# Eight scatters around the RMS factors split two and six, ranks inside the second layer, half a normed x moved to the head of the odd steps

## The chip, the cores and the metric

The kernel runs as one launch on one core of a Trainium2 chip. The metric is the time of one execution on the device in microseconds (us); smaller is better. The core's engines run side by side and meet only at semaphores: TensorE (PE: matrix products, with its weight loads shown as PEld), VectorE (DVE), ScalarE (ACT), GpSimd (POOL) and SyncE (SP, which only starts DMA transfers). Each engine works through its own instructions in order.

## What is computed

A layer norm, a graph layer with a residual, a second layer norm and a mixture of eight experts with a residual, for 8 batches of 1024 tokens of width 128:

```python
def gnn(x, adjacency, epsilon, W1, b1, rms_weight, W2, b2):
    agg = epsilon * x + einsum('bnm,bmd->bnd', adjacency, x)
    h = einsum('bnd,dh->bnh', agg, W1) + b1                 # hidden width 512
    h = silu(h * rsqrt(mean(h * h) + 1e-6) * rms_weight)
    return einsum('bnh,hd->bnd', h, W2) + b2

def ffn(x, Wg, bg, W1, b1, W2, b2):                         # 8 experts, 2 chosen for each token
    scores = einsum('bsd,ed->bse', x, Wg) + bg
    top, idx = top_k(scores, 2);  p = softmax(top)
    return sum over the two chosen e of p_e * (relu(x @ W1[e].T + b1[e]) @ W2[e].T + b2[e])

x = x + gnn(layernorm(x), adj, ...)
x = x + ffn(layernorm(x), ...)
```

## The kernel before

The 8192 tokens are cut into NG = 16 groups of 512 tokens (GT = 4 tiles of 128), two groups to a batch. The program has two parts. The **first part** does the graph layer and the choice of experts and ends with a scatter of every token's normed row to the two experts' places in the DRAM buffer `slots`. The **second part** takes `slots` in 71 tiles of 256 rows through the expert weights. The change touches only the first.

The first part is a software pipeline of 16 steps (`first_part`, `step(g, par, b)` on each engine, par = g % 2, b = g // 2). In step g, group g is multiplied by the adjacency (`M(0)` to `M(7)`, L545, eight pieces between which the other work of TensorE is laid), group g-1 goes through the hidden layer, group g-2 through the second layer norm, gate and ranks, and group g-3 is scattered. What one step does for group g-1 is a ring through all engines:

- VectorE adds the second layer's result of the group before into `x_all` (`add_second_layer`, L1079). I count a step from the start of one L1079 to the start of the next; step 10 is the one from 206.5 to 229.8 us.
- VectorE then takes the second layer norm's statistics (`ln2_stats`, L1018, L1023), adds b1 to the first layer's result (`add_b1`, L1003), and writes the normed rows (`normed_rows`, L1030), which TensorE transposes (`transpose_normed`, L502) for the gate (`gate`, L509).
- GpSimd turns the statistics into factors (`ln2_factors`, L850, L851: an addition and a power), sends four of the eight scatters of group g-3 (`scatter_rows`, L884), computes the RMS factors of group g-1 (`rms_factors`, again L850, L851) from ScalarE's sums of squares (`sum_squares`, L700), and sends the other four. Each scatter is followed by a piece of other work: in odd steps a fill (`rest_by_fill`, L871), in even steps one eighth of the addition of b2 to a batch of x (`rest_by_b2`, L877). At the end of an even step it computes the first layer norm's factors of the next batch (`ln1_factors`, L855 to L858).
- VectorE and ScalarE scale the hidden values, half each (`scale_hidden`, L1038, L705). TensorE transposes them (`transpose_hidden`, L495, 16 matmuls), ScalarE applies silu (`hidden`, L714), and TensorE does `M(6)`, the ranks (`rank`, L515 and L519, which wait for VectorE's choices), `M(7)` and the second layer (`second_layer`, L529, 32 matmuls).

ScalarE also makes the normed x of the next batch (`normalise`, L691) in the odd steps: one half behind `scale_hidden`, the other behind `hidden`; it waits for `ln1_factors`. It rounds the aggregate (L748) and, in steps 4 to 11, the high part of an expert's first weights (`high_weights`, L684), of which VectorE makes the low part (`low_weights`, L987) at the end of the same step, behind `add_second_layer`. The adjacency of group g+2 is loaded by SyncE (2 MB) when `M(7)` of group g is over. `normed_rows` and `places` wait until the scatters of the group two before, which used the same buffers, have landed.

## Time and profile before

| | |
|---|---|
| median of three runs | 653.26 us (652.2 to 655.01) |
| the profiled execution, whole | 647.74 us |
| its span, first to last instruction | 646.0 us |
| TensorE busy | 562.3 us (87%) |
| GpSimd busy | 408.7 us (63%) |
| VectorE busy | 352.0 us (54%) |
| ScalarE busy | 294.7 us (46%) |
| mean granted TensorE clock | 0.949 |

The profile comes from one execution. Its page gives the busy time of each engine, the chain of work that ended last (followed back from the last instruction through whatever released each step) and the costliest groups of instructions. The trace behind it can be asked for the waits, for the timeline of one engine and for the busy time and granted clock of any stretch. In a timeline row the first number is the start in us from the beginning of the span, the second the duration; "x4" means four instructions merged into the row; the bracket says how long the engine stood idle before and what released it.

### The profile page before, as it was taken

To read this page: it belongs to the slowest core of one execution; us is meant where nothing else is said; L and a number is where in the kernel's file an instruction comes from. 1 tells how busy PE (TensorE), PEld (TensorE's weight loads), DVE (VectorE), ACT (ScalarE), POOL (GpSimd) and SP (SyncE) were. 2 spreads that over 40 slices of the span, in tenths; PEclk is the share of its full clock that TensorE was granted. 3 is DMA by queue.
4 is the path that set the end of the run, shared out by engine and by line. 5 is a ranking of instruction groups with operands and counts; after the bars stand their busy time and mean duration, and the time that the engine had idled before them with its cause. 6 is when DMAs were issued, how large, how long until landed. Compare 5 with 4: busy or idle time off the path is not lost.

```text
span 646.0 us, 13035 instructions
## 1 busy us (share of the span) xinstructions
PE 562.3 (87%) x3704; PEld 463.3 (72%) x3704; DVE 352.0 (54%) x1174; ACT 294.7 (46%) x779; POOL 408.7 (63%) x664
## 2 busy tenths in 40 slices
PE   1999878978798789888985899999999999999882
PEld 0467655655466457555764889999999999999850
DVE  2566665765765757554636474445444444544454
ACT  3354544536345445363342345544554554455411
POOL 5244596477664864775566588776667667667750
PEclk9999879999998799889786899999999999999998
DMA  8995414432344134324010567766767666766698
GB/s 364 334 417 214 151 34 150 152 127 92 122 156 150 35 146 151 104 90 148 17 34 21 205 213 265 254 246 253 256 237 258 258 239 237 265 247 242 217 408 365
DMA packets 40519, 127.18 MB, mean 197 GB/s; under 512 B 7776, under 2 KB 19809, under 8 KB 38273
## 3 DMA queue, kind: packets, MB, share of 16 engines
q1 hardware_dynamic: 31232, 108.88, 45.8%
q0 software_dynamic: 8640, 16.93, 7.9%
q8 instruction: 32, 0.52, 0.3%
q10 hardware_dynamic: 576, 0.53, 0.3%
q14 instruction: 39, 0.31, 0.2%
HBM read 61.19 MB, written 24.02 MB: 132 GB/s over the span
## 4 chain that ended last, share of the span: by engine, by line
PE 57%; POOL 17%; issue 8%; DVE 7%; DMA 5%; ACT 4%; SPq 2%; POOLq 0%; ACTq 0%; DVEq 0%
POOL slots L884 10%; PE ps_y L529 9%; PE ps_y L651 8%; PE ps_g L651 8%; PE ps_agg L545 7%; PE ps_t L495 3%; PE ps_h L495 3%; POOL rms_rstd L851 2%; PE ps_agg L638 2%; PE ps_agg L637 2%; PE ps_h L637 2%; PE ps_h L641 2%; PE ps_agg L641 2%; PE ps_h L638 2%; PE ps_t L626 2%
## 5 line engine op out<-in xcount | busy, mean ns | idle before, releaser
L951 POOL DMA_INDIRECT parts<-adj_in x142 | 138.6, 976 | 68.8 <-ACT adj_in L796 52.4
L545 PE MATMUL ps_agg<-adj_in,xn_both 128*128 128x512 f32 x256 | 137.5, 638 | 13.0 <-ACT xn_both L691 13.0
L884 POOL DMA_INDIRECT slots<-rows,dest x128 | 132.0, 1032 | 23.4 <-issue 23.4
L796 ACT ACTIVATE adj_in<-adj_in,share 128x128 f32<-128x128 f32 x142 | 49.4, 395 | 117.3 <-issue 104.4
L700 ACT ACTIVATE hn<-hb 128x512 f32<-128x512 f32 x64 | 40.0, 625 | 83.4 <-DVE hb L1003 83.4
L651 PE MATMUL ps_y<-W2e,hb 128*128 x576 | 70.2, 275 | 0.8 <-issue 0.8
L1215 DVE TENSOR_TENSOR xe_split<-ps_t,xe_split 128x256 fp32r<-128x256 f32 x71 | 30.1, 425 | 73.5 <-ACT xe_split L778 71.3
L651 PE MATMUL ps_g<-W2e,hn 128*128 x560 | 68.1, 275 | 0.0
L651 PEld LDWEIGHTS ps_y<-W2e,hb 128*128 128x128 f32 x576 | 67.3, 192 | 1.0 <-issue 1.0
L545 PEld LDWEIGHTS ps_agg<-adj_in,xn_both 128*128 128x128 f32 x256 | 46.5, 207 | 29.5 <-issue 26.9
L651 PEld LDWEIGHTS ps_g<-W2e,hn 128*128 128x128 f32 x560 | 65.4, 191 | 0.0
L529 PEld LDWEIGHTS ps_y<-consts,siluT 128*128 128x128 f32 x512 | 59.6, 192 | 7.3 <-issue 7.3
L850 POOL TENSOR_TENSOR ve<-mv,ln_eps 128x4 f32<-128x4 f32 x16 | 3.2, 199 | 91.9 <-DVE mv L1023 91.9
L529 PE MATMUL ps_y<-consts,siluT 128*128 128x128 f32 x512 | 59.8, 275 | 0.0
L495 PE MATMUL ps_h<-ident,hn 128*128 128x128 f32 x128 | 23.1, 340 | 36.3 <-ACT hn L705 36.3
L495 PEld LDWEIGHTS ps_h<-ident,hn 128*128 128x128 f32 x128 | 18.5, 173 | 48.0 <-DVE hn L1038 47.5
L871 POOL MEMSET rest_of_pool<- 128x128 f32 x222 | 50.1, 226 | 0.2
L637 PE MATMUL ps_agg<-xe_split,wcur 128*128 128x256 f32 x142 | 45.7, 322 | 0.0
L1038 DVE TENSOR_SCALAR hn<-hb,rms_rstd 128x512 f32<-128x512 f32 x32 | 14.1, 483 | 54.5 <-POOL rms_rstd L851 54.5
L705 ACT ACTIVATE hn<-hb,rms_rstd 128x512 f32<-128x512 f32 x32 | 21.3, 713 | 44.5 <-POOL rms_rstd L851 44.5
L637 PE MATMUL ps_h<-xe_split,wcur 128*128 128x256 f32 x142 | 40.0, 282 | 0.0
L638 PE MATMUL ps_agg<-xe_split,wcur 128*128 128x256 f32 x142 | 39.9, 281 | 0.0
(179 smaller groups left out, 1242.0 us busy)
## 6 DMA issues: line engine op xcount, KB each, us to landing
wcur<-expert_w SPq DMA_DIRECT2D x71, 578.0 KB
adj_in<-in_adjT SPq DMA_DIRECT2D x16, 2048.0 KB, 8.4
adj_in<-slots SPq DMA_DIRECT2D x71, 130.0 KB
expert_w<-parts SPq DMA_DIRECT2D x8, 512.0 KB, 9.4
out<-x_all SPq DMA_DIRECT2D x8, 512.0 KB, 7.0
x_all<-in_x SPq DMA_DIRECT2D x1, 3072.0 KB, 23.8
parts<-adj_in POOLq DMA_INDIRECT x142
expert_w<-in_F1T SPq DMA_DIRECT2D x1, 2048.0 KB, 19.4
```

Of the source, the lines that this page charges most:

```text
L495: ins = pe.transpose(h_bank[c][:, j * P:(j + 1) * P], hn[:, j, c * P:(c + 1) * P], ident[:, :])
L529: ins = pe.matmul(ps_y[:, j * P:(j + 1) * P], siluT[:, c, j * P:(j + 1) * P], W2s[:, c, :], start=(c == 0 and j == 0), stop=(c == HC - 1 a ...
L545: ins = pe.matmul(ps_agg[par][:, :], xn[b % 2][:, m, :], adj_in[par][:, m, :], start=(m == 0), stop=(m == TPB - 1))
L637: pe.matmul(ps_1[c][:, 0:TILE], W1cur[ku][:, 0, cs], xeT_hi[ku % 2], start=True, stop=False)
L638: pe.matmul(ps_1[c][:, 0:TILE], W1cur[ku][:, 1, cs], xeT_hi[ku % 2], start=False, stop=False)
L651: ins = pe.matmul(ps_2[ku % 2][:, j * P:(j + 1) * P], hT[ku % 2][:, c, j * P:(j + 1) * P], of(W2e, expert)[:, c * D:(c + 1) * D], start=(c ...
L700: act.activation(hn[:, j, :], hb[:, j, :], ACT.Square, accum_out=ss[:, j:j + 1]).then_inc(s_ss, 1)
L796: ins = act.activation(ye[ku][:, j, :], yb[ku % 2][:, j, :], ACT.Copy, scale=share[ku][:, j:j + 1])
L871: pool.memset(pause[:, :], 0.0).then_inc(s_rest, 1)
L884: pool.indirect_dma_start(out=slots, out_offset=bass.IndirectOffsetOnAxis(ap=dest[q % 2][:, c, j:j + 1], axis=0), in_=rows[q % 2][:, c, j, ...
L951: pool.indirect_dma_start(out=parts, out_offset=bass.IndirectOffsetOnAxis(ap=goes[u % 8][:, j, :], axis=0), in_=ye[ku][:, j, :], in_offset ...
L1215: dve.tensor_tensor(xeT_lo[k % 2], ps_e[k % 2][:, 0:TILE], xeT_hi[k % 2].bitcast(FP32), ALU.subtract).then_inc(s_eTc, 1)
```

## The change

Five things are written in another order; no instruction is added or taken out.

1. GpSimd sends two scatters of group g-3 ahead of `rms_factors`, not four, and six behind it (steps 3 to 15).
2. TensorE does the ranks between the chunks 1 and 2 of the second layer, not between `M(6)` and `M(7)`.
3. ScalarE does the first half of `normalise` at the head of the odd steps, ahead of `sum_squares`, not behind `scale_hidden`.
4. VectorE does `places` behind the low part of the aggregate (L1121), not ahead of it.
5. VectorE does `low_weights` ahead of the low part of the aggregate, one step later (steps 5 to 12), not behind `add_second_layer` (steps 4 to 11).

```diff
--- before.py
+++ after.py
@@ -569,13 +569,15 @@
                     pe.wait_ge(s_hna, g)
                     transpose_hidden(g - 1, (0, 1, 2, 3))
                 M(6)
-                if has(g, 2):
-                    rank(g - 2)
                 M(7)
                 if has(g, 1):
                     if g == 1:
                         pe.wait_ge(s_const, 16)
-                    second_layer(g - 1, range(HC))
+                    second_layer(g - 1, (0, 1))
+                if has(g, 2):
+                    rank(g - 2)
+                if has(g, 1):
+                    second_layer(g - 1, (2, 3))
             first_part(pe, step, NG - 1)
 
             q = NG - 1
@@ -729,6 +731,8 @@
             act.activation(W1_hi[:, :], W1_raw, ACT.Copy).then_inc(s_W1h, 1)
 
             def step(g, par, b):
+                if par == 1 and has(g, -1):
+                    normalise(b + 1, 0)
                 if has(g, 1):
                     for j in range(GT):
                         sum_squares(g - 1, j)
@@ -736,8 +740,6 @@
                     normed(g - 2, ps_y)
                 if has(g, 1):
                     scale_hidden(g - 1)
-                if par == 1 and has(g, -1):
-                    normalise(b + 1, 0)
                 if has(g, 1):
                     for c in range(HC):
                         hidden(g - 1, c)
@@ -878,9 +880,9 @@
                 if n == TPB - 1:
                     ins.then_inc(s_xb, 1)
 
-            def scatter_rows(q, c, b=None):
-
-                for j in range(GT):
+            def scatter_rows(q, c, tiles, b=None):
+
+                for j in tiles:
                     pool.indirect_dma_start(
                         out=slots, out_offset=bass.IndirectOffsetOnAxis(ap=dest[q % 2][:, c, j:j + 1], axis=0),
                         in_=rows[q % 2][:, c, j, :], in_offset=None,
@@ -910,14 +912,16 @@
                     pool.sem_inc(s_turn, 1)
                     if not has(g, 3):
                         x_plus_b2(b)
+                own_b2 = b if par == 0 else None
                 if has(g, 3):
                     pool.wait_ge(s_dest, g - 2)
                     pool.wait_ge(s_row2, g - 2)
-                    scatter_rows(g - 3, 0, b if par == 0 else None)
+                    scatter_rows(g - 3, 0, (0, 1), own_b2)
                 if has(g, 1):
                     rms_factors(g - 1)
                 if has(g, 3):
-                    scatter_rows(g - 3, 1, b if par == 0 else None)
+                    scatter_rows(g - 3, 0, (2, 3), own_b2)
+                    scatter_rows(g - 3, 1, range(GT), own_b2)
                 if par == 0 and has(g, -2):
                     pool.wait_ge(s_mv1, b + 2)
                     ln1_factors()
@@ -930,17 +934,17 @@
             ln2_factors(q - 1)
             pool.wait_ge(s_dest, q - 1)
             pool.wait_ge(s_row2, q - 1)
-            scatter_rows(q - 2, 0)
-            scatter_rows(q - 2, 1)
+            scatter_rows(q - 2, 0, range(GT))
+            scatter_rows(q - 2, 1, range(GT))
             ln2_factors(q)
             pool.wait_ge(s_dest, q)
             pool.wait_ge(s_row2, q)
             for c in range(2):
-                scatter_rows(q - 1, c)
+                scatter_rows(q - 1, c, range(GT))
             pool.wait_ge(s_dest, q + 1)
             pool.wait_ge(s_row2, q + 1)
             for c in range(2):
-                scatter_rows(q, c)
+                scatter_rows(q, c, range(GT))
 
             def scatter_results(t, k):
                 if live(t, 2):
@@ -1115,15 +1119,15 @@
                     second_choice(g - 2)
                 if has(g, -1):
                     add_eps(g + 1)
-                if has(g, 2):
-                    places(g - 2)
+                if 5 <= g < 5 + E:
+                    low_weights(g - 5)
                 dve.wait_ge(s_aggh, g + 1)
                 dve.tensor_tensor(aggT_lo[:, :], ps_agg[par][:, :], aggT_hi[:, :].bitcast(FP32),
                                   ALU.subtract).then_inc(s_agg, 1)
+                if has(g, 2):
+                    places(g - 2)
                 if has(g, 1):
                     add_second_layer(g - 1)
-                if 4 <= g < 4 + E:
-                    low_weights(g - 4)
                 order.end()
             first_part(dve, step, NG - 1)
```

The instructions as each engine gets them follow. Line numbers of the new kernel are up to four higher than those of the old.

GpSimd, an even step: from the second layer norm's factors (rstd) over the scatters (DMA slots) and pieces of b2 (x_all) to the RMS factors (rms_var, rms_rstd). Before:

```order
L851 TENSOR_TENSOR rstd<-ve,minus_half 128x4
L884 DMA slots<-rows,dest 69376x130
L877 TENSOR_TENSOR x_all<-x_all,consts 128x128
L884 DMA slots<-rows,dest 69376x130
L877 TENSOR_TENSOR x_all<-x_all,consts 128x128
L884 DMA slots<-rows,dest 69376x130
L877 TENSOR_TENSOR x_all<-x_all,consts 128x128
L884 DMA slots<-rows,dest 69376x130
L877 TENSOR_TENSOR x_all<-x_all,consts 128x128
L850 TENSOR_TENSOR rms_var<-ss,rms_eps 128x4
L851 TENSOR_TENSOR rms_rstd<-rms_var,minus_half 128x4
```

Now:

```order
L853 TENSOR_TENSOR rstd<-ve,minus_half 128x4
L886 DMA slots<-rows,dest 69376x130
L879 TENSOR_TENSOR x_all<-x_all,consts 128x128
L886 DMA slots<-rows,dest 69376x130
L879 TENSOR_TENSOR x_all<-x_all,consts 128x128
L852 TENSOR_TENSOR rms_var<-ss,rms_eps 128x4
L853 TENSOR_TENSOR rms_rstd<-rms_var,minus_half 128x4
L886 DMA slots<-rows,dest 69376x130
L879 TENSOR_TENSOR x_all<-x_all,consts 128x128
L886 DMA slots<-rows,dest 69376x130
L879 TENSOR_TENSOR x_all<-x_all,consts 128x128
```

The two instructions of the RMS factors stand two scatters and two pieces of b2 earlier; these four follow them.

ScalarE, an odd step: hn,ss is the sum of squares, xn2T the copy for the gate, hn the scaling of the hidden values, xn_both the normed x, siluT the silu; the row expert_w ends the step before. Before:

```order
L684 ACTIVATE expert_w<-expert_w 128x512
L700 ACTIVATE hn,ss<-hb 128x512 x4
L720 ACTIVATE xn2T<-ps_y 128x512
L705 ACTIVATE hn<-hb,rms_rstd 128x512 x2
L691 ACTIVATE xn_both<-x_all,shift,rstd 128x128 x4
L714 ACTIVATE siluT<-ps_h,consts 128x512 x2
L714 ACTIVATE siluT<-ps_t,consts 128x512 x2
L691 ACTIVATE xn_both<-x_all,shift,rstd 128x128 x4
L748 ACTIVATE aggT<-ps_agg 128x512
```

Now:

```order
L686 ACTIVATE expert_w<-expert_w 128x512
L693 ACTIVATE xn_both<-x_all,shift,rstd 128x128 x4
L702 ACTIVATE hn,ss<-hb 128x512 x4
L722 ACTIVATE xn2T<-ps_y 128x512
L707 ACTIVATE hn<-hb,rms_rstd 128x512 x2
L716 ACTIVATE siluT<-ps_h,consts 128x512 x2
L716 ACTIVATE siluT<-ps_t,consts 128x512 x2
L693 ACTIVATE xn_both<-x_all,shift,rstd 128x128 x4
L750 ACTIVATE aggT<-ps_agg 128x512
```

The first four instructions on xn_both stand ahead of the sums of squares, directly at the head of the step.

VectorE, the end of an even step and the head of the next: adj_in is the addition of epsilon, place, base, picked and dest are `places`, aggT is the low part of the aggregate, x_all is `add_second_layer`, expert_w is `low_weights`, st and mv are the statistics. Before:

```order
L1054 SCALAR_TENSOR_TENSOR rows<-is_high,result_row 128x8
L997 TENSOR_TENSOR adj_in<-adj_in,eps_ident 128x128 x4
L1063 TENSOR_TENSOR place<-ps_g,base 128x32
L1065 TENSOR_TENSOR base<-base,ps_g 128x8
L1066 TENSOR_TENSOR picked<-onehot,place 128x64
L1071 TENSOR_REDUCE dest<-picked 128x8
L1121 TENSOR_TENSOR aggT<-ps_agg,aggT 128x512
L1079 TENSOR_TENSOR x_all<-ps_y,x_all 128x512
L987 TENSOR_TENSOR expert_w<-expert_w 128x512
L1018 BN_STATS st<-x_all 128x6 x4
```

Now:

```order
L1058 SCALAR_TENSOR_TENSOR rows<-is_high,result_row 128x8
L1001 TENSOR_TENSOR adj_in<-adj_in,eps_ident 128x128 x4
L991 TENSOR_TENSOR expert_w<-expert_w 128x512
L1125 TENSOR_TENSOR aggT<-ps_agg,aggT 128x512
L1067 TENSOR_TENSOR place<-ps_g,base 128x32
L1069 TENSOR_TENSOR base<-base,ps_g 128x8
L1070 TENSOR_TENSOR picked<-onehot,place 128x64
L1075 TENSOR_REDUCE dest<-picked 128x8
L1083 TENSOR_TENSOR x_all<-ps_y,x_all 128x512
L1022 BN_STATS st<-x_all 128x6 x4
```

Between x_all and st nothing stands any more; expert_w and aggT now come before `places`.

## Rows read from the trace of the kernel before

**Rows 1.** The page's part 4: the last chain, shares of the span by line.
```profile
POOL slots L884 10%; PE ps_y L529 9%; PE ps_y L651 8%; PE ps_g L651 8%; PE ps_agg L545 7%; PE ps_t L495 3%; PE ps_h L495 3%; POOL rms_rstd L851 2%; PE ps_agg L638 2%; PE ps_agg L637 2%; PE ps_h L637 2%; PE ps_h L641 2%; PE ps_agg L641 2%; PE ps_h L638 2%; PE ps_t L626 2%
```

**Rows 2.** Waits over the span: engine, line, waited for: us in total, times, longest.
```profile
DVE hn L1038 <- POOL rms_rstd L851: 54.5, 14, 5.0
...
PE ps_h L495 <- ACT hn L705: 36.3, 14, 3.0
```

**Rows 3.** Windows: stretch, length, busy us (instructions) per engine, PEclk, DMA share, GB/s.
```profile
38.40:55.70 17.30, 16.84 (x94) 11.81 (x93) 13.70 (x61) 8.03 (x17) 7.34 (x9) 1.00 0.95 363
...
142.90:162.60 19.70, 17.04 (x94) 11.73 (x93) 11.87 (x46) 11.59 (x26) 12.48 (x20) 1.00 0.40 134
...
185.10:206.50 21.40, 18.64 (x94) 13.37 (x93) 11.90 (x45) 11.81 (x26) 12.54 (x20) 0.92 0.35 124
...
206.50:229.80 23.30, 19.45 (x94) 13.60 (x94) 15.89 (x62) 8.99 (x18) 16.71 (x24) 0.85 0.32 115
...
318.00:339.00 21.00, 18.66 (x94) 12.84 (x93) 10.59 (x40) 8.45 (x17) 12.51 (x20) 0.92 0.08 27
```

**Rows 4.** Timeline of VectorE, step 10: start us, us, engine, line, operation [idle before <-releaser].
```profile
206.53 0.69 DVE L1079 TENSOR_TENSOR x_all<-ps_y,x_all 128x512 f32<-128x512 f32 x1 [2.16 <-PE ps_y L529]
207.14 0.68 DVE L987 TENSOR_TENSOR expert_w<-expert_w 128x512 fp32r<-128x512 f32 x1
...
212.21 1.29 DVE L1030 TENSOR_SCALAR rows<-x_all,mv,rstd 128x128 f32<-128x128 f32 x4
```

**Rows 5.** Timeline of GpSimd, step 10.
```profile
209.10 0.20 POOL L850 TENSOR_TENSOR ve<-mv,ln_eps 128x4 f32<-128x4 f32 x1 [7.37 <-DVE mv L1023]
...
213.99 1.00 POOL L884 DMA_INDIRECT slots<-rows,dest  x1 [0.16 <-issue]
...
215.65 1.00 POOL L884 DMA_INDIRECT slots<-rows,dest  x1 [0.17 <-issue]
...
217.09 0.21 POOL L850 TENSOR_TENSOR rms_var<-ss,rms_eps 128x4 f32<-128x4 f32 x1
217.38 1.04 POOL L851 TENSOR_TENSOR rms_rstd<-rms_var,minus_half 128x4 f32<-128x4 f32 x1
...
227.62 0.20 POOL L858 TENSOR_TENSOR shift<-zeros,ve 128x8 f32<-128x8 f32 x1
```

**Rows 6.** Timeline of TensorE, steps 7, 9 and 10.
```profile
155.10 1.06 PE L495 MATMUL ps_h<-ident,hn 128*128 128x128 f32 x8 [2.53 <-ACT hn L705]
...
193.62 1.10 PE L545 MATMUL ps_agg<-adj_in,xn_both 128*128 128x512 f32 x2
...
197.39 1.81 PE L495 MATMUL ps_h<-ident,hn 128*128 128x128 f32 x8 [2.67 <-ACT hn L705]
...
213.56 0.66 PE L502 MATMUL ps_y<-ident,rows 128*128 128x128 f32 x4 [0.84 <-DVE rows L1030]
...
215.82 1.10 PE L545 MATMUL ps_agg<-adj_in,xn_both 128*128 128x512 f32 x2
...
219.93 1.94 PE L495 MATMUL ps_h<-ident,hn 128*128 128x128 f32 x8 [3.01 <-ACT hn L705]
```

**Rows 7.** Timeline of GpSimd, step 9.
```profile
192.03 0.98 POOL L884 DMA_INDIRECT slots<-rows,dest  x1 [0.16 <-issue]
...
193.39 0.98 POOL L884 DMA_INDIRECT slots<-rows,dest  x1 [0.17 <-issue]
...
194.55 0.21 POOL L850 TENSOR_TENSOR rms_var<-ss,rms_eps 128x4 f32<-128x4 f32 x1
```

**Rows 8.** Windows, same columns: the transposes of step 10.
```profile
219.90:223.60 3.70, 3.67 (x17) 3.70 (x18) 3.34 (x12) 2.06 (x3) 3.32 (x5) 0.50 0.11 36
```

**Rows 9.** Timeline of ScalarE, step 9: half a batch normed.
```profile
197.15 1.63 ACT L691 ACTIVATE xn_both<-x_all,shift,rstd 128x128 f32<-128x128 f32 x4
```

**Rows 10.** The page's part 5: the sums of squares on ScalarE.
```profile
L700 ACT ACTIVATE hn<-hb 128x512 f32<-128x512 f32 x64 | 40.0, 625 | 83.4 <-DVE hb L1003 83.4
```

**Rows 11.** The last chain in order of time: start us, us, what.
```profile
386.89 4.01 DMA slots<-rows,dest
```

## The prediction

> **What bounds the kernel now.** I read the last chain by line first, then the waits, then windows cut at the edges of the steps, then the timelines of one even and one odd step. The chain names GpSimd's scatters, L884, as its largest line [rows 1]: an engine that is busy 63% of the span has the largest share of what ends last. The waits say where: VectorE waits 54.5 us in 14 places for the RMS factors, and TensorE 36.3 us for the hidden values scaled with them [rows 2]. That is the first part. The second part runs at its own rate and is not touched.
>
> The windows give the size: steps 3 to 15, all that have scatters, last from 55.7 to 339.0 us, 283.3 us in all; an odd one 21.4, an even one 23.3. Step 2, without scatters, takes 17.3 with TensorE busy for 16.84 of it and the clock at 1.00 [rows 3]. That is the floor.
>
> The ring in step 10, counted from L1079 at 206.53: GpSimd takes the statistics at 209.10, sends four scatters 1.66 us apart, and reaches rms_var only at 217.09 [rows 4, 5]. TensorE starts the hidden transposes at 219.93, 2.84 us behind rms_var, after 3.01 us of idle time; its earlier work was done at 215.82 + 1.10 = 216.92 [rows 6]. In step 9 the same: scatters 1.36 apart [rows 7], rms_var at 194.55, transposes at 197.39 (again 2.84), idle 2.67. So the four scatters ahead of the RMS factors are on the path.
>
> **The change part by part.** In step coordinates (0 = L1079).
>
> *Two scatters moved behind.* They take 2 x 1.66 = 3.3 us from the ring in even steps, 2 x 1.36 = 2.7 in odd ones.
>
> *low_weights moved.* L987 stands between L1079 and the statistics, 0.6 us on the ring in steps 4 to 11 [rows 4]. At its new place VectorE stood idle before (2.16 us ahead of L1079 [rows 4]), so I count it nothing there. In the steps without weights there is nothing to win; an even one then ends up to 0.6 later than I write below, 10.4 + 7.5 in place of 9.8 + 7.5 at the worst (steps 4, 14).
>
> *Even step.* rms_var: 217.09 - 206.53 = 10.56, less 0.6, less 3.3: 6.6. Transposes possible at 6.6 + 2.84 = 9.5. But TensorE's own work ended at 216.92 - 206.53 = 10.4; it waits 0.84 us for the normed rows [rows 6], which VectorE brings 0.6 earlier without L987: 9.8. TensorE is now the later one by 0.3, and the transposes start at 9.8, not 13.4. *Odd step:* rms_var at 194.55 - 185.10 = 9.45, less 0.6, less 2.7: 6.1, transposes possible at 9.0; TensorE's own work ends at 193.62 + 1.10 - 185.10 = 9.6.
>
> *From the transposes to the end of the step* I take the clock into account. Step 9 needs 206.5 - 197.39 = 9.1 us, step 7 needs 162.6 - 155.10 = 7.5 for the same instructions [rows 3, 6]: step 7 has the clock at 1.00, steps 9 and 10 have 0.92 and 0.85, and in the transposes of step 10 it is 0.50 [rows 3, 8], the lower of its two levels (1.2 of 2.4 GHz), after idle 3.01 us. The clock sometimes holds over such a wait (step 7, idle 2.53) and sometimes not. With a wait of a few tenths, as in step 2, I take the full clock: 7.5. The bounds are 7.5 and 9.1.
>
> The Trainium skill, "TensorE: Matmul & The Clock Gate", section "What's actually happening", says of the loss that "for modeling, the ramp penalty is <1% of a typical kernel span"; by it at most 6.5 us of 646 would come back. The trace speaks against it: of the windows of the 13 steps eleven show 0.85 or 0.92 (three of them are in [rows 3]), at about 1.6 us each some 18 us. What the page's figure would make of the sum stands with the rivals.
>
> *Ranks inside the second layer.* The same five matmuls, later; a wait for the choices ahead of `M(7)` can go. The 7.5 of step 7 is taken without such a wait, and I count nothing more. `places` must now follow ranks that come in the middle of the second layer; its four small operations have VectorE's idle time ahead of L1079, 2.16 us in step 10 [rows 4], to stand in. If they did not fit, L1079 would be late by what sticks out, some tenths.
>
> So an **even step takes 9.8 + 7.5 = 17.3** and an undisturbed odd one 9.6 + 7.5 = 17.1. Is another engine late then? VectorE is busy 15.9 of 23.3 us in step 10 [rows 3]: it fits in 17.3 with 1.4 to spare. GpSimd in an even step ends with the first layer norm's factors at 227.62 + 0.20 = 21.3 after L1079, now 20.7 (0.6 less; the two scatters only change sides). The step is over at 17.3. So **GpSimd runs 3.4 us into the next odd step**, and there the third edit bites: ScalarE stands at the head of that step waiting for these factors, norms its half batch (1.63 us [rows 9]) until 5.0, and only then takes the squares, 40.0 / 16 = 2.5 us a group [rows 10], until 7.5. With a handover rms_var comes at 7.7, not 6.1; GpSimd's own chain (the statistics at 3.4, then 217.09 - 209.10 = 8.0 us to rms_var in step 10, less 4 x 0.3 for the shorter pieces of an odd step, less 2.7) would give 7.5. Transposes at 7.7 + 2.84 = 10.5, the step 10.5 + 7.5 = **18.1 us** (rounded up). This applies to the odd steps 5 to 13; step 3 follows a step without scatters and step 15 one without the norm's factors.
>
> *The normed half's old place* (step 9, 197.15) is beside the transposes; leaving it wins nothing, since the silus are not what the second layer waits for. In step 1 the new place may hold the squares up, once, by up to 1.6 us; I take 0.5.
>
> *Six scatters behind instead of four* are beside VectorE's choices. The Trainium skill, "DMA: Bandwidth & Descriptors", section "SWDGE vs HWDGE vs iDMA", says that VectorE locks GpSimd out of the memory in its two-port modes, where the descriptors of such scatters are written; by it more scatters would be lengthened. An estimate from it: if the 26 moved scatters took a quarter longer each (1.00 us one [rows 5]), the ring would lose at most 26 x 0.25 = 6.5 us.
>
> **The sum.** Steps 4, 6, ... 14: 6 x 17.3 = 103.8. Steps 5 to 13: 5 x 18.1 = 90.5. Steps 3 and 15: 2 x 17.1 = 34.2. Together 228.5 against 283.3: 54.8 less; with step 1, **54.3 us less**. From 339.0 on the chain starts at the same L1079 with the same instructions and comes earlier as a whole. The profiled execution took 647.7 us (span 646.0 and 1.7 around it) and would take 593.4; it lies 5.6 under the median of the runs, 653.3. I subtract from the median: **599 us**.
>
> **The rivals.**
>
> *The clock does not come back.* For: in 11 of 13 steps it is low now, and there remain shorter waits (for the normed rows, the gate, in odd steps some tenths for the hidden values). Against: step 7 and step 2. Even 9.8 + 9.1 = 18.9; odd 9.6 + 9.1 = 18.7, since GpSimd then is only 1.8 us late and nobody waits. 6 x 18.9 + 7 x 18.7 = 244.3, 39 us less: **614**.
>
> *It comes back in half of the steps.* Waits that fall now at 1.00, now at 0.92 (steps 7 and 9) speak for it. Half of the 15 us between 614 and 599: **607**. The page's one per cent, 39 + 6.5 us less, would give 608.
>
> *The late scatters land late.* In an even step rms_rstd now starts at 6.9 and takes 1.3 with its handover, so the sixth scatter behind it starts at 8.2 + 5 x 1.66 = 16.5. From issue to landing one took 4.01 us [rows 11], so it lands 3.2 us into the odd step, where VectorE overwrites the buffer with the next normed rows at about 5.7 (212.21 - 206.53 [rows 4]). But the load of an adjacency group, which starts when `M(7)` is over and ahead of the second layer, now starts while the last of them are on their way. If landing takes twice as long, the rows come 1.7 late and the odd steps lose 1 to 1.7: **606**.
>
> *GpSimd is not late.* If ScalarE's squares and GpSimd's tail fit, all steps are at the floor: 7 x 17.1 + 6 x 17.3 = 223.5, 60 less: **593**.
>
> *Slower: the loop over the norm's factors.* The head of the odd step holds ScalarE until six scatters and the factors are through. If each of the six with its piece of b2 took 4 us, not 1.66, beside the choices and the adjacency load, the squares would be 14 us later in five odd steps: 70 us more than I forecast, **669**. It decides from 3.6 us apiece, where 57 us are lost; nothing in the trace comes near.
>
> *It does not do what it says.* If the squares on ScalarE and not the scatters set the RMS factors, only L987 counts: **650**. Against: GpSimd has no idle time ahead of rms_var [rows 5, 7].
>
> **How the numbers follow.** Main case 0.61 (595 to 603), clock stays low 0.12, comes back by half 0.05, late landing 0.09, floor 0.08, slower 0.03, no effect 0.02. The range takes in the clock's rival, whose term has the widest bounds, and the floor, with 2 or 3 us beyond each since the profiled execution lies 5.6 from the median: 590 to 616. A measurement of this kernel tells about 0.5% from no change; faster by more than that 0.95, within it 0.02, slower 0.03.
>
> **What would show it.** Steps of 17 to 18.5 us between starts of L1079; PEclk 1.00 from step 3 to 15; the wait of TensorE for the scaled hidden values (36.3 us) nearly gone in even steps, some tenths in odd ones; ScalarE waiting for `shift` of the norm's factors at the head of odd steps; GpSimd without idle time over an even step's end. Even steps near 19 with PEclk 0.9 show the clock's rival; VectorE's L1030 waiting for a DMA shows the landing. Wrong would be the whole reading if rms_var came with GpSimd idle ahead of it in even steps.

## The result and the profile after

The changed kernel takes **594.91 us** (median of 4 runs, 594.13 to 599.59), the kernel before 652.73 (median of 4, 651.22 to 655.01); the ratio is 0.9126, 95% interval 0.908 to 0.9172. The time lies in the predicted range (590 to 616), 4 us under the forecast of 599. The profiled execution of after took 599.59 us (span 597.6); it is the longest of its four, where that of before lay 5.0 us under the median of its four. So the medians differ by 57.8 us, and the two traces, which are what can be explained, by 48.2 (spans: 48.4). The remaining 9.7 us are between one execution and another, and no trace shows them. Here and below a ratio compares only the executions within 1.5% of the fastest of their kernel, so where the executions of one kernel lie further apart it can differ from the quotient of the medians.

Part 4 of the page, shares of the span in the chain that ended last; the scatters still lead it [rows 1], and pieces of b2 (L879) and the landing of scatters are new among its largest lines. Lines of the changed kernel are up to four higher:

```profile
POOL slots L886 9%; PE ps_y L653 9%; PE ps_g L653 8%; PE ps_agg L545 7%; PE ps_y L529 6%; POOL x_all L879 3%; DMA slots<-rows,dest 3%; PE ps_agg L640 2%; PE ps_agg L639 2%; PE ps_t L628 2%; ACT hn L702 2%; PE ps_h L639 2%; PE ps_agg L643 2%; PE ps_h L643 2%; PE ps_h L640 2%
```

The waits (engine, line, waited for: us in total, times, longest). VectorE's wait for the RMS factors was 54.5 us in 14 places and TensorE's for the scaled hidden values 36.3 us [rows 2]:

```profile
ACT xn_both L693 <- POOL shift L860: 35.1, 7, 6.6
...
DVE hn L1042 <- POOL rms_rstd L853: 20.2, 9, 3.0
...
PE ps_h L495 <- ACT hn L707: 2.4, 5, 0.9
```

TensorE's wait is down by 34 us. The first line is the new wait at the head of the odd steps.

Windows of steps 2, 10 and 11 (stretch, length, busy us (instructions) of PE, PEld, DVE, ACT, POOL, then PEclk, DMA share, GB/s), against [rows 3]:

```profile
39.42:56.71 17.29, 16.82 (x94) 11.88 (x93) 13.77 (x61) 9.57 (x21) 7.33 (x9) 1.00 0.92 355
...
181.42:198.62 17.20, 16.83 (x94) 11.89 (x93) 16.06 (x63) 8.67 (x18) 13.35 (x19) 1.00 0.44 157
198.62:218.72 20.10, 18.85 (x94) 13.30 (x93) 12.15 (x45) 11.72 (x26) 16.13 (x26) 0.92 0.40 136
```

Step 10 now has the length of step 2, with TensorE busy for 16.83 of 17.20 us: the floor. Step 11 is 2.9 us longer, at a lower clock. All thirteen steps, from the starts of L1079 and L1083, in us:

| step | 3 | 4 | 5 | 6 | 7 | 8 | 9 | 10 | 11 | 12 | 13 | 14 | 15 | sum |
|---|---|---|---|---|---|---|---|---|---|---|---|---|---|---|
| before | 21.1 | 23.0 | 21.5 | 21.6 | 19.7 | 22.5 | 21.4 | 23.3 | 21.3 | 22.5 | 21.0 | 23.3 | 21.1 | 283.4 |
| after | 17.0 | 17.2 | 18.2 | 17.9 | 17.4 | 17.2 | 19.9 | 17.2 | 20.1 | 17.2 | 18.4 | 17.9 | 16.9 | 232.4 |

The even step first, TensorE in step 10 (timeline: start us, us, engine, line, operation, then [idle before <-releaser]). The transposes start 191.17 - 181.42 = 9.75 us into the step, not 13.4, and with no wait; the second row is the end of the ranks, now inside the second layer [rows 6]:

```profile
191.17 1.04 PE L495 MATMUL ps_h<-ident,hn 128*128 128x128 f32 x8
...
196.45 0.24 PE L519 MATMUL ps_g<-both,ones 128*128 128x32 bf16 x4
```

GpSimd over the end of step 10 and into step 11 [rows 5, 7]. Step 11 begins at 198.62:

```profile
188.19 0.21 POOL L852 TENSOR_TENSOR rms_var<-ss,rms_eps 128x4 f32<-128x4 f32 x1
...
198.56 1.00 POOL L886 DMA_INDIRECT slots<-rows,dest  x1 [0.16 <-issue]
199.59 0.47 POOL L879 TENSOR_TENSOR x_all<-x_all,consts 128x128 f32<-128x128 f32 x1
...
202.33 0.20 POOL L860 TENSOR_TENSOR shift<-zeros,ve 128x8 f32<-128x8 f32 x1
202.50 0.20 POOL L852 TENSOR_TENSOR ve<-mv,ln_eps 128x4 f32<-128x4 f32 x1
...
206.75 0.20 POOL L852 TENSOR_TENSOR rms_var<-ss,rms_eps 128x4 f32<-128x4 f32 x1
```

rms_var comes 6.8 us into the even step, not 10.6. The last scatter of step 10 is sent as step 11 begins, and the norm's factors (shift) are done 202.53 - 198.62 = 3.9 us into it. It then takes the second layer norm's factors and sends the odd step's two scatters without idle time but for the issues, and reaches rms_var 8.1 us into the step. What ScalarE and TensorE do with that in step 11 [rows 6, 9]:

```profile
202.57 1.65 ACT L693 ACTIVATE xn_both<-x_all,shift,rstd 128x128 f32<-128x128 f32 x4 [6.09 <-POOL shift L860]
...
208.10 1.33 ACT L707 ACTIVATE hn<-hb,rms_rstd 128x512 f32<-128x512 f32 x2 [0.95 <-POOL rms_rstd L853]
```

```profile
205.12 0.66 PE L502 MATMUL ps_y<-ident,rows 128*128 128x128 f32 x4 [0.32 <-DVE rows L1034]
207.20 1.06 PE L509 MATMUL ps_g<-consts,xn2T 128*128 128x8 f32 x8 [0.57 <-ACT xn2T L722]
209.58 1.63 PE L495 MATMUL ps_h<-ident,hn 128*128 128x128 f32 x8 [0.36 <-ACT hn L707]
211.00 1.91 PE L495 MATMUL ps_t<-ident,hn 128*128 128x128 f32 x8
```

The transposes start 11.0 us into the odd step after three waits of 0.3 to 0.6 us, and take 1.63 and 1.91 us where they took 1.04 in step 10: the granted clock was 0.55 over them (209.6 to 212.7 us), the lower of its two levels for nearly all of that time. From there to the end of the step it is 218.72 - 209.58 = 9.1 us, not 7.5.

### The profile page after: what moved, and what is told of

Read it like the earlier page. It is cut to its first block, busy times and chain, and to the rows that moved or that the text cites. A ratio compares the mean times of both kernels' runs of the same rounds, so it can differ in the third digit from the quotient of the medians.

```text
span 597.6 us, 13049 instructions
## 1 busy us (share of the span) xinstructions
PE 546.7 (91%) x3704; PEld 452.7 (76%) x3704; DVE 353.6 (59%) x1174; ACT 291.7 (49%) x779; POOL 408.9 (68%) x664
## 4 chain that ended last, share of the span: by engine, by line
PE 54%; POOL 17%; DMA 8%; issue 8%; DVE 5%; ACT 5%; SPq 3%; POOLq 0%; ACTq 0%; DVEq 0%
POOL slots L886 9%; PE ps_y L653 9%; PE ps_g L653 8%; PE ps_agg L545 7%; PE ps_y L529 6%; POOL x_all L879 3%; DMA slots<-rows,dest 3%; PE ps_agg L640 2%; PE ps_agg L639 2%; PE ps_t L628 2%; ACT hn L702 2%; PE ps_h L639 2%; PE ps_agg L643 2%; PE ps_h L643 2%; PE ps_h L640 2%
## 5 line engine op out<-in xcount | busy, mean ns | idle before, releaser
L886 POOL DMA_INDIRECT slots<-rows,dest x128 | 132.2, 1033 | 23.4 <-issue 23.2
L545 PE MATMUL ps_agg<-adj_in,xn_both 128*128 128x512 f32 x256 | 128.8, 611 | 12.9 <-ACT xn_both L693 12.9
L529 PE MATMUL ps_y<-consts,siluT 128*128 128x128 f32 x512 | 62.8, 277 | 0.0
L639 PE MATMUL ps_agg<-xe_split,wcur 128*128 128x256 f32 x142 | 45.8, 323 | 0.0
L693 ACT ACTIVATE xn_both<-x_all,shift,rstd 128x128 f32<-128x128 f32 x64 | 26.2, 487 | 35.1 <-POOL shift L860 35.1
L639 PE MATMUL ps_h<-xe_split,wcur 128*128 128x256 f32 x142 | 40.0, 282 | 0.0
L640 PE MATMUL ps_agg<-xe_split,wcur 128*128 128x256 f32 x142 | 39.9, 281 | 0.0
L643 PE MATMUL ps_h<-xe_split,wcur 128*128 128x256 f32 x142 | 39.9, 281 | 0.0
L640 PE MATMUL ps_h<-xe_split,wcur 128*128 128x256 f32 x142 | 39.7, 280 | 0.0
L643 PE MATMUL ps_agg<-xe_split,wcur 128*128 128x256 f32 x142 | 39.7, 280 | 0.0
## 6 DMA issues: line engine op xcount, KB each, us to landing
expert_w<-parts SPq DMA_DIRECT2D x8, 512.0 KB, 10.6
expert_w<-in_F1T SPq DMA_DIRECT2D x1, 2048.0 KB, 18.6
```

The source lines that it names most:

```text
L529: ins = pe.matmul(ps_y[:, j * P:(j + 1) * P], siluT[:, c, j * P:(j + 1) * P], W2s[:, c, :], start=(c == 0 and j == 0), stop=(c == HC - 1 a ...
L545: ins = pe.matmul(ps_agg[par][:, :], xn[b % 2][:, m, :], adj_in[par][:, m, :], start=(m == 0), stop=(m == TPB - 1))
L639: pe.matmul(ps_1[c][:, 0:TILE], W1cur[ku][:, 0, cs], xeT_hi[ku % 2], start=True, stop=False)
L640: pe.matmul(ps_1[c][:, 0:TILE], W1cur[ku][:, 1, cs], xeT_hi[ku % 2], start=False, stop=False)
L643: pe.matmul(ps_1[c][:, 0:TILE], W1cur[ku][:, 0, cs], xeT_lo[ku % 2], start=False, stop=True).then_inc(s_l1, 1)
L886: pool.indirect_dma_start(out=slots, out_offset=bass.IndirectOffsetOnAxis(ap=dest[q % 2][:, c, j:j + 1], axis=0), in_=rows[q % 2][:, c, j, ...
```

## The experiments

They ran on three other chips of this kind, one for each group of runs below. The kernel before takes some 40 us longer on them (medians of 690.67, 701.03 and 689.74 us), and every trace taken there has it behind the steps: from the end of step 15 to the end of the span it is 339 to 360 us in the eleven traces, against 307 before and 308 after on the first chip. So I compare the steps, which the change is about, read from each kernel's one trace. They repeat better: the one kernel that ran on two of these chips had 225.9 and 226.0 us in the steps, and 357 and 339 behind them. The kernel before has a trace on the first chip alone. Per kernel, in us:

| kernel | even steps | odd steps 5 to 13 | steps 3 to 15 |
|---|---|---|---|
| before, first chip | 21.6 to 23.3 | 19.7 to 21.5 | 283.4 |
| change, first chip | 17.2 to 17.9 | 17.4 to 20.1 | 232.4 |
| change, other chip | 17.1 to 17.2 | 19.1 to 19.8 | 235.0 |
| four and four | 22.8 to 23.3 | 21.0 | 286.1 |
| normed half in old place | 17.2 to 17.6 | 18.5 to 19.0 | 232.1 |
| split alone | 17.8 to 18.9 | 17.2 to 18.1 | 232.0 |
| b2 over both steps | 17.0 to 17.8 | 16.9 to 18.1 | 226.5 |
| the same, step 1 as before | 17.0 to 17.7 | 16.9 to 18.2 | 225.9; again 226.0 |
| that split and b2 alone | 17.5 to 18.4 | 17.0 to 18.0 | 226.3 |
| change, ranks early | 17.7 to 18.6 | 17.1 to 18.0 | 230.6 |
| change, waits filled | 17.2 | 19.1 to 19.4 | 234.6 |
| before, waits filled | 21.2 to 21.7 | 19.5 to 19.8 | 266.7 |

### First group: which edit does it

**Four and four.** The changed kernel with four scatters ahead and four behind.

```diff
-                    scatter_rows(g - 3, 0, (0, 1), own_b2)
+                    scatter_rows(g - 3, 0, range(GT), own_b2)
                 if has(g, 1):
                     rms_factors(g - 1)
                 if has(g, 3):
-                    scatter_rows(g - 3, 0, (2, 3), own_b2)
                     scatter_rows(g - 3, 1, range(GT), own_b2)
```

> The changed kernel with its first edit alone undone: four scatters ahead of the RMS factors and four behind; the other four edits stay. My theory: the scatters ahead are what the step hangs on, so nearly all of the gain goes. rms_var comes 3.3 us (even) or 2.7 us (odd) later, TensorE waits 2 to 3 us for the scaled hidden values again and the clock falls again in most steps: even steps 21 to 22 us, odd ones 20 to 21, the whole 640 to 648 us. Rival (the other four edits carry the gain, through VectorE's shorter way to the statistics and the ranks): below 625 us.

Measured: 693.62 us (683.81 to 699.48) against 690.67 by the medians, ratio 1.0294 to the kernel before on that chip, interval 1.0168 to 1.042, by which it is unclear whether it is slower; steps 3 to 15 in 286.1 us. The whole gain is gone, and more than I had expected with the other edits in place (21 to 22 us in even steps, 20 to 21 in odd ones). Windows of steps 9 and 10, and TensorE's transposes in step 10:

```profile
187.60:208.60 21.00, 18.67 (x94) 13.13 (x93) 11.99 (x46) 10.53 (x22) 12.57 (x20) 0.92 0.35 124
208.60:231.90 23.30, 19.93 (x94) 13.92 (x93) 16.23 (x63) 10.64 (x22) 17.13 (x24) 0.85 0.32 116
```

```profile
221.51 1.94 PE L495 MATMUL ps_h<-ident,hn 128*128 128x128 f32 x8 [3.00 <-ACT hn L707]
```

The wait of 3.00 us is back, and the clock of the kernel before with it (0.92 and 0.85). Moving L987 takes 0.5 us from the way to the transposes (221.51 - 208.60 = 12.9 for 13.4), and it comes back behind them, where `M(6)` and `M(7)` run at the low clock (3.12 us for the four matmuls that take 1.88 in step 10 of the change).

**The normed half in its old place.** The changed kernel with the call behind `scale_hidden` again.

```diff
             def step(g, par, b):
-                if par == 1 and has(g, -1):
-                    normalise(b + 1, 0)
...
                     scale_hidden(g - 1)
+                if par == 1 and has(g, -1):
+                    normalise(b + 1, 0)
```

> The changed kernel with its third edit alone undone: the first half of the normed x is made behind the scaling again, not at the head of the odd steps. The trace of the changed kernel shows GpSimd 3.3 to 4 us late in the odd steps and ScalarE waiting at their head. Theory A, as my prediction has it: the head of the step costs 0.2 us an odd step beside GpSimd's own lateness, which stays: 592 to 595 us, no difference. Theory B: it is ScalarE's wait and half batch that lengthen the odd steps; without them they take 1.3 to 3 us less: 582 to 588 us.

Measured: 639.57 us (614.97 to 647.18), steps 3 to 15 in 232.1 us. No gain from it worth the name. In step 11 of the change ScalarE ends its squares at 206.67, and GpSimd, late by itself, reaches rms_var at 206.75. Here the squares of step 11 end at 5.9 us into the step, 2.1 earlier, and yet rms_var comes at 7.93 for 8.13 and the transposes start at 10.78 for 10.96: 0.2 us, as the forecast has it. Both chains are nearly equally late, and taking one away leaves the other. The step lengths themselves are no measure of it, since a delay ahead of `place`, shown further down, is in them too.

**The split alone.** The kernel before with nothing but the two scatters moved.

```diff
...
-                    scatter_rows(g - 3, 0, b if par == 0 else None)
+                    scatter_rows(g - 3, 0, b if par == 0 else None, (0, 1))
                 if has(g, 1):
                     rms_factors(g - 1)
                 if has(g, 3):
+                    scatter_rows(g - 3, 0, b if par == 0 else None, (2, 3))
                     scatter_rows(g - 3, 1, b if par == 0 else None)
```

> The kernel before with the first edit alone: two scatters ahead, six behind; the other four edits left out. Theory: this one edit brings nearly the whole gain; left out are 0.6 us of the low weights where TensorE does not cover them (even steps 4 to 10) and the wait for the choices ahead of the last piece of the adjacency product (0.3 to 0.6 us): 598 to 604 us. Rival: the edits need each other (the choices are late for the ranks once the hidden values come early, and TensorE waits there): above 612 us.

Measured: 642.24 us (635.55 to 647.55), ratio 0.9286, interval 0.9169 to 0.9404; steps 3 to 15 in 232.0 us. Against four and four on the same chip that is 54 us less. The split alone brings all of it, which I had not expected; I had the other edits worth some us. They do shift time between the steps. TensorE in step 10 of this kernel, which begins at 180.69, with L987 (here L988) still behind `add_second_layer`:

```profile
188.13 0.66 PE L502 MATMUL ps_y<-ident,rows 128*128 128x128 f32 x4 [1.53 <-DVE rows L1031]
...
191.34 1.04 PE L495 MATMUL ps_h<-ident,hn 128*128 128x128 f32 x8
```

The transposes start 10.65 us into the step against 9.75 with all edits. In steps 6, 8 and 12 the difference is 0.5 us, so that much, and not 0.9, goes with the place of L987. The ranks in their old place cost another 0.1 to 0.7 us behind the transposes. In the odd steps, though, this kernel has 17.2 to 18.1 us at a full clock, no more than the change. So what the four other edits win in even steps (4.6 us in six) is lost again in odd ones (5.1 in five, 3.4 of them the clock): a shorter even step does not shorten GpSimd's work, and shift, done 3.4 us into step 11 here, is done at 3.9 in the change.

**b2 over both steps.** The changed kernel with GpSimd's work evened out: from step 6 on an even step keeps four of its eight pieces of b2, and the odd step before takes the other four in the place of fills.

```diff
-                    if b is None:
+                    if b is None or c * GT + j not in pieces:
                         rest_by_fill()
...
-                own_b2 = b if par == 0 else None
+                own_b2, pieces = (b, range(4, 8)) if par == 0 else (None, ())
+                if g == 4:
+                    pieces = range(8)
...
-                    scatter_rows(g - 3, 1, range(GT), own_b2)
+                    if par == 1 and 5 <= g < NG - 1:
+                        pool.wait_ge(s_xn, 2 * b + 3)
+                        scatter_rows(g - 3, 1, range(GT), b + 1, range(4, 8), 4)
+                    else:
+                        scatter_rows(g - 3, 1, range(GT), own_b2, pieces)
```

> The changed kernel with the pieces of b2 spread: four of a batch's eight pieces (0.47 us each, a fill in their old place takes 0.22) stand in the odd step before, so GpSimd is done with an even step 1.0 us earlier. Theory (GpSimd's lateness sets the odd steps 5 to 13): each of five odd steps 1.0 us shorter, and the clock may hold in those where it fell: 586 to 591 us. Rival (the odd steps are set by the landing of the scatters or by TensorE): 594 to 596 us, no change.

Measured: 638.88 us, ratio 0.9204, interval 0.9119 to 0.9289; steps 3 to 15 in 226.5 us, 6.0 less than the change. GpSimd around the start of step 11, which is at 196.05 here:

```profile
198.86 0.20 POOL L860 TENSOR_TENSOR shift<-zeros,ve 128x8 f32<-128x8 f32 x1
...
203.29 0.21 POOL L852 TENSOR_TENSOR rms_var<-ss,rms_eps 128x4 f32<-128x4 f32 x1
```

shift is done 3.0 us into the odd step, not 3.9, rms_var at 7.2, not 8.1, and the transposes start at 10.1, not 11.0. Step 5, behind a step 4 that keeps all its pieces, is the control: 18.1 us, as in the change. It is GpSimd's lateness that sets when the transposes of an odd step start. Not all of the 6.0 us is that: over steps 5 to 13 the earlier transposes are 2.9 us, and 3.4 are the clock, which fell in steps 9 and 11 of the change and in none here.

### Second group: the clock, the change once more, the best version

**The kernel before with the wait filled.** TensorE does 24 transposes that nobody reads ahead of the hidden transposes, so that it does not stand idle while it waits.

```diff
                 M(5)
+                if g >= 3:
+                    keep_busy(ps_agg[1 - par], 24)
                 if has(g, 1):
                     pe.wait_ge(s_hn, g)
```

> The kernel before with 24 idle transposes (2.8 us) ahead of the hidden transposes in steps 3 to 15, where TensorE waits 2.3 to 3.0 us for the scaled values. It prices the clock by itself. Theory: PEclk 1.00 in all steps, each of the eleven steps that had the lower clock 1.6 us shorter, steps 3 to 15 take 264 to 269 us in place of 283.4, the whole 15 to 18 us less. Rival (the page's one per cent, or the lower clock hidden by other engines): 277 to 284 us, at most 6.5 us less.

Measured: 678.83 us (670.8 to 684.81), ratio 0.9699, interval 0.9527 to 0.9872; steps 3 to 15 in 266.7 us, 16.7 less, with every other instruction where it was. Steps 9 and 10, then TensorE in step 9:

```profile
179.80:199.50 19.70, 19.57 (x118) 14.41 (x117) 11.96 (x46) 11.59 (x26) 12.48 (x20) 1.00 0.34 119
199.50:221.10 21.60, 19.78 (x118) 14.29 (x117) 15.69 (x62) 8.67 (x18) 16.80 (x24) 1.00 0.38 138
```

```profile
189.31 2.78 PE L537 MATMUL ps_agg<-ident 128*128 128x128 f32 x24
192.01 1.07 PE L495 MATMUL ps_h<-ident,hn 128*128 128x128 f32 x8
192.92 1.04 PE L495 MATMUL ps_t<-ident,hn 128*128 128x128 f32 x8
```

The granted clock is 1.00 in both, and the transposes take 1.07 and 1.04 us where they took 1.81 and 1.91 after the wait. The transposes start where they did (12.2 and 13.4 us into the steps, 12.3 and 13.4 before), so all of it lies behind them. That is against the kernel before on the first chip; on this one the kernel before has no trace, but its whole time is 22 us above this kernel's by the medians, and the kernel with four and four, on another of the chips, has 286.1. Of the 51 us that the steps lose by the change, 32 are the earlier start of the transposes. Some 13 are the clock: these 16.7 less the 3.4 us that steps 9 and 11 of the change still pay. The other 5 or so are the wait for the choices ahead of `M(7)` in the even steps, which the ranks' new place removes: from the transposes to the end 8.2 us in step 6 before, at a full clock, and 7.45 now.

**The change again, and with its short waits filled.** The second kernel puts five idle transposes ahead of the gate and three ahead of the hidden transposes, in odd steps from 5.

```diff
                 M(4)
+                if par == 1 and g >= 5:
+                    keep_busy(ps_agg[1 - par], 5)
                 if has(g, 2):
                     gate(g - 2)
                 M(5)
+                if par == 1 and g >= 5:
+                    keep_busy(ps_agg[1 - par], 3)
```

> The changed kernel as it is, beside the other runs on one chip. Steps 3 to 15 take 229 to 236 us by the starts of the addition into x (232.4 in its first trace, 283.4 in the kernel before); the spread is the clock, which fell in two odd steps of the first trace, for 1.7 us each. Both theories below expect this.

> The changed kernel with idle transposes (5 ahead of the gate, 3 ahead of the hidden transposes, about 0.115 us each) in the odd steps 5 to 15, where TensorE waits 0.6 and 0.4 us. Theory (the short waits still let the clock fall in odd steps): PEclk 1.00 in every step, odd steps 5 to 13 between 17.4 and 18.4 us, none near 20; steps 3 to 15 take 227 to 230 us. Rival (the fall does not hang on these waits): odd steps near 20 us remain somewhere, and the fill costs up to 0.3 us a step, 232 to 236 us.

Measured: 649.78 us (635.8 to 652.18) and steps in 235.0 us for the change; 646.45 us, ratio 0.932, interval 0.9222 to 0.9418, and steps in 234.6 with the waits filled. What this was made for it could not show: on this chip the change has a clock below 1.00 in step 5 alone (0.91, and 1.00 with the waits filled, one step of each), so there was hardly anything to fill. And yet steps 7 to 13 of the change take 19.1 to 19.3 us with the clock at 1.00. Their transposes start as on the first chip (10.9 us into step 11). The rest comes at their end. VectorE at the end of step 11 of the change, and the ranks on TensorE:

```profile
216.25 0.69 DVE L1125 TENSOR_TENSOR aggT<-ps_agg,aggT 128x512 fp32r<-128x512 f32 x1 [1.09 <-ACT aggT L750]
218.76 0.19 DVE L1067 TENSOR_TENSOR place<-ps_g,base 128x32 f32<-128x32 f32 x1 [1.83 <-remote]
219.46 0.68 DVE L1083 TENSOR_TENSOR x_all<-ps_y,x_all 128x512 f32<-128x512 f32 x1
```

```profile
216.37 0.24 PE L519 MATMUL ps_g<-both,ones 128*128 128x32 bf16 x4
216.47 2.03 PE L529 MATMUL ps_y<-consts,siluT 128*128 128x128 f32 x16
```

`place`, the first operation of `places`, waits for the ranks. The last rank matmul is over at 216.61 in the trace, but `place` starts at 218.76, when the second half of the second layer has ended too (218.50), and `add_second_layer` (L1083) follows it without a pause, some 0.9 us behind the end of what it adds. The release has no instruction in the trace ("remote"). This delay costs steps 7 to 13 some 0.9 us each.

**Step 1 put back.** The kernel with b2 over both steps, and the normed half of step 1 alone in its old place.

```diff
-                if par == 1 and has(g, -1):
+                if par == 1 and g > 1 and has(g, -1):
                     normalise(b + 1, 0)
...
+                if g == 1:
+                    normalise(b + 1, 0)
```

> The changed kernel with b2 spread as in the run before, and the half normed x of step 1 alone behind the scaling again. Steps 3 to 15 as with b2 spread, 226 to 228 us; step 1 ends 1.0 us earlier, since ScalarE's squares of group 0 no longer wait for the norm's factors: some 6 to 8 us less than the change, 587 to 590 us where the change takes 595. Rival (step 1 is held by the load of the adjacency group that add_eps waits for): no gain in step 1.

Measured: 639.04 us (624.75 to 644.99); steps 3 to 15 in 225.9 us, 9.1 less than the change has on the same chip, where the medians differ by 10.7. Of the 9.1 the earlier transposes of steps 5 to 13 are 4.1, the clock of step 5 is 1.7, and most of the rest is the delay ahead of `place`, which these steps no longer show. Step 15 ends at 281.6 us, against 290.6 in the change on this chip and 289.1 on the first. Step 1 ends at 38.42, 1.1 us earlier than in the kernel of the first group (39.54). But the change, with the half batch at the head of step 1, ends it at 38.29 on this chip, so the edit is not what the 1.1 us are; the cause is taken up with step 1 below.

### Third group: what the four other edits are worth

**The ranks in their old place.** The changed kernel with `rank` between `M(6)` and `M(7)`.

```diff
                 M(6)
+                if has(g, 2):
+                    rank(g - 2)
                 M(7)
...
-                    second_layer(g - 1, (0, 1))
-                if has(g, 2):
-                    rank(g - 2)
-                if has(g, 1):
-                    second_layer(g - 1, (2, 3))
+                    second_layer(g - 1, range(HC))
```

> The changed kernel with the ranks back between M(6) and M(7), the other edits kept. Theory A: in odd steps of the changed kernel on the second chip VectorE's place (L1067) starts about 2 us after the ranks are done and L1083 comes 1 us late with it; that delay belongs to the ranks' late place. With the ranks early, place starts without a wait, odd steps go from 19.2 to about 18.2, steps 3 to 15 from 235 to 230. Theory B: the delay belongs to VectorE's place itself or to the head of the step, and the ranks' place makes no difference: 234 to 236. On a chip that does not show the delay: within 1 us of 232.4 by both, even steps up to 0.2 longer for the wait for the choices.

Measured: 633.13 us (629.72 to 645.55), ratio 0.9211, interval 0.9046 to 0.9376; steps 3 to 15 in 230.6 us. Here `place` follows L1123 without a wait in every odd step, as here at the end of step 5, whose ranks ended at 103.34:

```profile
105.62 0.69 DVE L1123 TENSOR_TENSOR aggT<-ps_agg,aggT 128x512 fp32r<-128x512 f32 x1 [1.09 <-ACT aggT L748]
106.22 0.18 DVE L1065 TENSOR_TENSOR place<-ps_g,base 128x32 f32<-128x32 f32 x1
```

Odd steps take 17.1 to 18.0 us, even ones 17.7 to 18.6. As the first theory said (230 us), the ranks inside the second layer cost more in odd steps than they bring in even ones, on a chip that shows the delay: 235.0 against 230.6. But the two traces come from different chips, and the first chip shows no delay of that kind: there `place` starts 0.04 us behind the ranks where it waits for them. A part of the shorter odd steps is also only the longer even ones ahead of them: shift is done 2.4 to 3.2 us into these odd steps, 2.9 to 3.9 in the change.

**The split and b2 alone.** The kernel before with the split and with b2 over both steps, by the lines shown above, and none of the other edits.

> The kernel before with two things only: two scatters ahead of the RMS factors and six behind, and the b2 pieces of steps 6, 8, ... dealt half to the odd step before. The other four edits of the change are left out. Theory A (the four edits bring nothing once GpSimd is on time): steps 3 to 15 as in the kernel with all edits and the spread pieces, 226 us, within 1.5 us either way, and step 1 as before, x_all of step 1 at 38.4. Theory B (places and low_weights in their old order and the ranks ahead of M(7) stand on the path of the even steps once the odd ones are short): even steps 17.8 to 18.3, steps 3 to 15 230 to 233 us.

**The best once more**, in the same group:

> The changed kernel with the b2 pieces of steps 6, 8, ... dealt half to the odd step before and the half batch of step 1 normed in its old place, once more, beside the two others of this call. Steps 3 to 15 226 us as measured before, or up to 227; 6 to 7 us below the changed kernel in the first part and 1 us in step 1; as a whole 587 to 590 us where the second part runs as in the kernel before on the first chip, 636 to 642 where it is 40 us longer in every kernel.

Measured: 629.68 us (611.99 to 631.61) and steps in 226.3 us without the four edits; 629.12 us (621.15 to 642.87) and steps in 226.0 with them; the kernel before in this group 689.74 (680.25 to 701.49). With GpSimd on time the four edits again make no difference. In the kernel without the four edits steps 3 to 15 are 57 us shorter than before, 6 more than by the change. Neither was run on the first chip.

## Why the prediction was right, and where not

**The bound, the mechanism: right.** Four scatters ahead of the RMS factors were on the path. The run with four and four gives back the whole gain, the run with the split alone has all of it.

**The even step: right.** 9.8 + 7.5 = 17.3 forecast; 9.75 + 7.45 = 17.20 in step 10, the clock at 1.00. Steps 4, 8, 10 and 12 are at 17.20 or 17.21. Step 4, where I allowed 0.6 more without the weights, has nothing more. The six even steps sum to 104.6 us for 103.8.

**The late landing: partly right.** Steps 6 and 14 take 17.9. VectorE's normed rows in step 6, which begins at 109.03:

```profile
114.60 1.60 DVE L1034 TENSOR_SCALAR rows<-x_all,mv,rstd 128x128 f32<-128x128 f32 x4 [0.28 <-DMA slots<-rows,dest]
```

They wait 0.28 us for a scatter to land, start 0.4 us later in the step than in step 10 and take 1.60 us for 1.29 there. The last of step 5 was sent at 107.45, 7.1 us earlier. Such waits stand in steps 6, 7 and 14 (0.28, 0.17 and 0.39 us), and in the last chain of the changed kernel the landings behind the latter two stand with their lengths:

```profile
125.83 6.40 DMA slots<-rows,dest
252.76 7.13 DMA slots<-rows,dest
```

The 4.01 us of [rows 11] that I reckoned with was a poor reference: that scatter was sent at 386.89, behind the last step, and at the same place the changed kernel has 3.57. What a landing takes between the steps of the kernel before, no row shows. The rival asked what would be if landing took twice as long, and 6.4 to 7.1 us are nearly that. (By its own terms the rows would come 1.5 us late, not 1.7: 16.5 + 8.0 - 17.3 = 7.2 for 5.7.) It costs less than the rival's 1 to 1.7 us in each odd step: one odd step waits 0.17 us, and two of six even steps, whose rows wait for scatters sent at the end of the odd step, are some 0.7 longer. The waits do belong to the split: the three kernels with four scatters on either side have none of them, and every kernel with two and six has one to four.

**The odd step: the mechanism right, a term missed.** Forecast: GpSimd 3.4 us late, rms_var at 7.7, transposes at 10.5, the step 18.1. In step 11: 3.9, 8.1, 11.0. Steps 5, 7 and 13, with the clock at 1.00, take 18.2, 17.4 and 18.4, on average 18.0. Steps 9 and 11 take 19.9 and 20.1. **The step of the prediction that failed is "with a wait of a few tenths, as in step 2, I take the full clock: 7.5".** In step 11 three waits of together 1.25 us stood ahead of the transposes, in step 9 two of 0.92, and the clock went to its lower level there (1.2 of 2.4 GHz); the way to the end took 9.1 us, the upper bound that I had given. Why there and not in step 13 behind the same waits, no run shows. The clock's rival, written for all steps, holds in two of thirteen. The five steps sum to 94.0 for 90.5, 3.5 more, of which these two ways to the end are 3.3. That the clock alone makes a step longer by some 1.5 us is shown by the kernel before with its wait filled; that filling these short waits would hold the clock was tried on a chip where it held anyhow, and stays open.

The order of ScalarE was named as what bites in the odd step, and GpSimd's own chain only as giving 0.2 less. The runs bear that small difference out: with the normed half moved back the transposes start 0.2 us earlier, with GpSimd's tail shortened 0.9. Edit 3 is harmless because GpSimd is late anyway.

**Step 1: nothing of it is the third edit.** 0.5 us forecast, 1.0 measured (step 1 ends at 39.42, before at 38.38). But the values that the squares need come later themselves. The additions of b1 in step 1, before and then now:

```profile
26.08 1.39 DVE L1003 TENSOR_TENSOR hb<-ps_t,consts 128x512 f32<-128x512 f32 x2 [0.86 <-PE ps_t L490]
```

```profile
27.14 1.39 DVE L1007 TENSOR_TENSOR hb<-ps_t,consts 128x512 f32<-128x512 f32 x2 [0.86 <-PE ps_t L490]
```

The third square waits 0.83 us for this one in both kernels, so the half batch at the head holds nothing up. Some 0.8 of the 1.06 us are there already in the first adjacency product (18 matmuls in 10.87 us for 10.02), ahead of anything that the edits move. With the half batch at the head step 1 ends at 38.3 in three of six traces and at 39.4 to 39.6 in three; with it in the old place at 38.2 to 38.8 in seven. What makes that first product longer stays open.

**The rest of the kernel: mis-sized.** "From 339.0 on comes earlier as a whole": from that L1079 to the end of the span it was 306.96 us, now 597.6 - 289.14 = 308.46, 1.5 more, 0.4 of it in the last group's step and 1.1 behind it. I did not follow that further.

**The sum.** Steps 3.9 short of the forecast saving (even 0.8, odd 5 to 13 3.5, steps 3 and 15 -0.3), step 1 0.5, the rest 1.5: 5.9 us. The forecast span was 646.0 - 54.3 = 591.7, and 591.7 + 5.9 = 597.6. I had then raised the sum by 5.6 us for the distance of the profiled execution of before from its median. The one of after lies on the other side of its own, by 4.7. That the median comes out 4 us under my 599 is this scatter and not a better kernel than forecast. In the traces 6 us less are saved than forecast, in the medians 4 more; that the whole time comes so close to 599 is in part luck.

**The other four edits.** I gave moving L987 0.6 us a step on the ring in both kinds of step and the ranks nothing. In even steps of the run with the split alone the first is 0.5 us in three and the second 0.1 to 0.7. In odd ones GpSimd is late anyhow, and later by what the even step is shorter, which I had not set against the gain. Over all steps the four edits bring nothing (232.0 without them, 232.4 and 235.0 with them), and also nothing once GpSimd is on time (226.3 and 226.0).

**The slow clock.** The kernel before with its wait filled is 16.7 us faster in these steps, 2.6% of its 646; the prediction's working had some 18. The Trainium skill, "TensorE: Matmul & The Clock Gate", section "What's actually happening", puts the ramp below one per cent of a typical kernel's span. It says so of the warm-up, and the prediction took it for all that the clock costs, at most 6.5 us here. For a kernel whose TensorE waits 2.2 to 3.1 us in each of 13 steps the measurement decides against that figure. The rival built on it (608) was wrong for that reason.

**The scatters beside VectorE.** The six behind took 1.24, 1.00, 1.00, 1.00, 1.26 and 1.00 us in step 10, on the mean 1.08 for 1.00. By the Trainium skill, "DMA: Bandwidth & Descriptors", section "SWDGE vs HWDGE vs iDMA", VectorE can lock GpSimd out; over the whole first part 128 scatters are 1033 ns on the mean in the changed kernel, 1026 ns with four and four and 1032 in the kernel before. The trace shows no loss that counts.

## What to carry to other kernels

When one engine deals out small pieces of work around a handover that a ring waits for, count what stands ahead of the handover, and put no more there than the ring's other wait hides; then look at where the pieces go that are moved behind it, because they make that engine late for its next handover. Even such work out over the steps before reordering anything else: here that brought 6 us against the change on the first chip and 9 on another, 3 to 4 of them by the earlier handover itself, and four further edits together brought nothing. A wait of TensorE costs its own length and, with the clock at its lower level behind it, nearly half as much again (here 36.3 us over the span and 16.7).
